# Two attention blocks and a feed-forward on one core: x and context in fp16 parts, a gate buffer of its own, feed-forward in two halves

## The chip, the core and the metric

The kernel runs on one core of a Trainium2 chip. A core has five engines that run their own instruction streams and meet at semaphores: TensorE (matmuls, PE in the profile, its weight loads PEld), VectorE (DVE), ScalarE (ACT), GpSimd (POOL) and SyncE (SP), which here only issues DMAs. The metric is the device time of one launch in microseconds. It is best read as a median of several runs; the profile is one execution of its own.

## What is computed

64 sequences of 128 tokens (x, 320 channels) with a context of 192 channels. Block L0 is attention with 8 heads to the context, plus a small attention over four tokens, with a residual. Block L1 is a transformer layer: self attention with 20 heads, cross attention to the context, and a gated feed-forward.

```python
def L0(x, enc, Wq, Wk, Wv, Wq_ca, Wk_ca, Wv_ca, Wout, b_out):
    keys, ca = enc[:, :-4], enc[:, -4:]
    hs = mha(x @ Wq, keys @ Wk, keys @ Wv)                 # 8 heads
    ca_q1 = einsum('btc,th->bch', ca, Wq_ca)[:, indices]
    ca_hs1 = mha(ca_q1, x, x)
    ca_hs2 = mha(ca_hs1 @ Wq, ca @ Wk_ca, ca @ Wv_ca)
    return (hs + ca_hs2) @ Wout + b_out + x
def L1(x, context):
    h = ln1(x); x = attn(h @ q1, h @ k1, h @ v1) @ o1 + b1 + x     # 20 heads
    h = ln2(x); x = attn(h @ q2, context @ k2, context @ v2) @ o2 + b2 + x
    a, g = split(ln3(x) @ ff_w1 + ff_b1)
    return a * gelu(g) @ ff_w2 + ff_b2 + x
```

## The kernel before

Two sequences (256 columns) make a step; there are 32 steps and a loop of 33 passes (Fori in each engine's block: L475 for SyncE, L587 GpSimd, L805 ScalarE, L1278 VectorE, L1709 TensorE). The passes are a pipeline: pass i does L0 of step i, and the L1 layer of the step before it, and within that feed-forward lags by another part. A tail after the loop does the last feed-forward.

The work is cut into **jobs**, named in the table BODY (L109). A job fills one of six PSUM banks (j_bank, handed round in the table's order), then ScalarE, VectorE or both read it (A, V, AV), and the bank is free for the job six places on. The same order is written out by hand in each engine's loop. Names: Q0T, K0T and V0 project x and context for L0 (three chunks of output channels, or one job per sequence for V), K1T, Q1T, V1 and Q2T, K2T, V2 for L1; Sn are the scores of unit n (four heads), of which VectorE takes maxima; mxg turns the maxima of group g; Tn are the transposed scores less the maxima, of which ScalarE takes two exponentials: P in fp32 (L741) and PT's high part in fp16 (L742). GpSimd forms PT's low part P - PT (low_probabilities, L514), and TensorE's attend n (L1549) multiplies both with V in two other banks. There are 28 units a pass: 0 to 3 the token attention (CA), 4 to 13 self, 14 to 23 cross, 24 to 27 the first attention. P has two slots, PT three (P_SLOTS, PT_SLOTS). outT/outM turn and project an attention's result, followed by residual, statistics, the deviation on GpSimd and norm; XT turns a normed row. fft (t 0 to 9) are the feed-forward's first products, of which ScalarE takes Gelu into gate (L715) and VectorE multiplies into F; y0 and y1 the second product, in parts (ff_part, L1612). G, mT, mB, vca, s4, p4T, hs, caT belong to the token attention and to the scale factors, which are powers of two found afresh in each pass from the largest elements of x and context.

**Precision.** A product in fp16 parts splits both factors into a high and a low part and takes the products high-high, high-low and low-high. With 320 rows of contraction these are eight matmuls (PASSES, L36: the last 64 rows and their low part share one block). Only products of normed rows and weights do so; x and context enter Q0T, K0T, V0, K2T, V2 as fp32: chunk (L1460, through transposed, L1429) takes three fp32 matmuls for x and two for context, values (L1471) two per job. In the trace each fp32 matmul is two instructions.

**Operands on SyncE's queue.** Queries and keys go through DRAM: put writes the two parts of a chunk to a scratch, stack (L373) loads them back with three DMAs, one copy per part pair. SyncE issues in the order of one_pass (L430), and a wait there holds up all that follows. stack_self feeds units 4 to 13, stack_cross_keys and stack_cross_queries units 14 to 23, stack_first_* units 24 to 27. load_next (L423) loads the next step's inputs; cT2 keeps the context for K2T and V2.

**The gate** lies in slot 0 of P (L285). So Gelu 0 waits for the last low part of self attention (L715 and on), and the exponential of unit 14 waits for ff9.

The head (L1143 to L1276 on VectorE) loads and splits the weights, finds their scale, and makes the token attention's products M4.

## Time and profile before

| | us |
|---|---|
| median of 3 runs | 3948.45 |
| lowest, highest | 3946.22, 3966.26 |
| the profiled execution | 3965.49 |
| span of its trace | 3963.6 |
| its mean granted clock | 0.966 |

How to read it: busy time is the union of an engine's instructions. Matmuls are pipelined, so the distance from one start to the next is a matmul's price, and its own length (some 0.2 us for a single one) is not. A granted clock of 1.00 is 2.4 GHz for TensorE and 0.50 is 1.2 GHz. An arrow names what ended an engine's idle time before an instruction.

### The profile page before, as it was taken

The numbers are of one execution on the slowest core, as the hardware profiler recorded it, in microseconds if no ns is written. First come the engines' busy times: TensorE is split into PE (matmuls) and PEld (weight loads), VectorE is DVE, ScalarE is ACT, GpSimd is POOL, SyncE is SP. The second block draws the span as 40 slices with busy tenths as digits, with TensorE's granted clock in tenths as the row PEclk, the third lists the DMA queues.
The fourth block names the chain that finished last, engine by engine and source line by source line (L and its number), as shares of the span: only waits on it lengthen the run. The fifth ranks groups of instructions, "written<-read, shape, count | busy, mean of one in ns | idle before, by whom it ended". The sixth has DMA issues, their size and how long they took to land.

```text
span 3963.6 us, 112057 instructions
## 1 busy us (share of the span) xinstructions
PE 3580.9 (90%) x38314; PEld 2867.6 (72%) x38314; DVE 2308.9 (58%) x5535; ACT 2268.7 (57%) x4084; POOL 1966.4 (50%) x2229
## 2 busy tenths in 40 slices
PE   6499999999999999999999999999999999999999
PEld 5377777777777777777777777777777777777777
DVE  6466556556555655655556556555655656556555
ACT  2356655665556556556655665566566556655664
POOL 0345444554555445555554554545445555554553
PEclk9799999999999999999999999999999999999999
DMA  4332333222233332232333322233332232333321
GB/s 138 63 61 53 58 61 66 59 46 60 59 55 61 67 61 49 53 65 51 63 63 66 59 46 60 56 58 61 67 64 47 53 64 53 63 63 66 59 46 42
DMA packets 417600, 238.71 MB, mean 60 GB/s; under 512 B 44315, under 2 KB 416715, under 8 KB 416843
## 3 DMA queue, kind: packets, MB, share of 16 engines
q1 hardware_dynamic: 405317, 229.62, 29.6%
q8 instruction: 366, 6.00, 0.7%
q10 hardware_dynamic: 11910, 3.04, 0.3%
q14 instruction: 7, 0.06, 0.0%
HBM read 153.50 MB, written 79.06 MB: 59 GB/s over the span
## 4 chain that ended last, share of the span: by engine, by line
PE 36%; issue 30%; POOL 17%; DVE 5%; SPq 4%; DMA 3%; ACT 3%; POOLq 1%; ACTq 0%; DVEq 0%
PE bank L1412 35%; POOL PT L519 10%; DMA xin<-in_x 3%; DVE mx L1025 2%; ACT PT L742 2%; POOL cQ L526 2%; POOL XA L496 1%; POOL cK L526 1%; SPq L365 1%; POOL rstd L566 1%; SPq L363 1%; POOL XB L496 1%; PE bank L1446 1%; PE bank L1531 1%; SPq L361 1%
## 5 line engine op out<-in xcount | busy, mean ns | idle before, releaser
L519 POOL TENSOR_TENSOR PT<-P,PT 128x512 f16<-128x512 f32 (+1 forms) x924 | 1068.8, 1157 | 642.1 <-ACT PT L742 640.8
L1412 PE MATMUL bank<-hT,w_ff_w 128*128 128x256 f16 x5440 | 651.6, 277 | 1.7 <-DVE hT L1054 1.7
L1025 DVE TENSOR_REDUCE mx<-bank 128x4 f32<-128x512 f32 (+1 forms) x924 | 579.6, 680 | 104.4 <-PE bank L1412 96.5
L1412 PEld LDWEIGHTS bank<-hT,w_ff_w 128*128 128x128 f16 x5440 | 532.5, 100 | 73.2 <-issue 6.5
L1412 PE MATMUL bank<-mxs,pick 84*128 84x128 f16 (+1 forms) x3696 | 513.4, 220 | 0.0
L1412 PE MATMUL bank<-w_ff,F 128*128 128x320 f32 x1360 | 411.5, 442 | 1.3 <-DVE F L1104 1.3
L1412 PEld LDWEIGHTS bank<-mxs,pick 84*128 84x128 f16 (+1 forms) x3696 | 375.1, 103 | 16.8 <-issue 8.2
L1412 PEld LDWEIGHTS bank<-V,PT 128*128 128x128 f16 (+1 forms) x9504 | 314.5, 96 | 84.0 <-POOL PT L519 37.9
L723 ACT ACTIVATE P<-bank,ff_b,scale 128x256 f32<-128x256 f32 x340 | 187.8, 562 | 324.9 <-PE bank L1412 285.4
L1412 PE MATMUL bank<-Qs,Ks 96*128 96x128 f16 x2640 | 361.7, 220 | 0.1
L1412 PE MATMUL bank<-V,PT 128*128 128x17 f16 (+1 forms) x9504 | 343.7, 172 | 17.1 <-POOL PT L519 14.3
L1104 DVE SCALAR_TENSOR_TENSOR F<-bank,ff_b,P 128x256 f32<-128x256 f32 x340 | 163.3, 483 | 266.5 <-ACT P L723 262.7
L741 ACT ACTIVATE P<-bank,log_p,held 128x512 f32<-128x512 f32 x330 | 256.2, 776 | 80.7 <-PE bank L1412 42.8
L1412 PEld LDWEIGHTS bank<-w_ff,F 128*128 128x128 f32 x1360 | 242.4, 190 | 78.0 <-DVE F L1104 1.5
L565 POOL TENSOR_TENSOR rstd<-mv,eps 128x1 f32<-128x1 f32 x198 | 41.4, 209 | 502.8 <-DVE mv L1092 502.8
L741 ACT ACTIVATE P<-bank,log_p,exp_self 128x512 f32<-128x512 f32 x330 | 255.6, 775 | 45.0 <-PE bank L1412 42.8
L1412 PEld LDWEIGHTS bank<-Qs,Ks 96*128 96x128 f16 x2640 | 253.2, 98 | 20.9 <-issue 6.0
L1071 DVE RECIPROCAL rden<-bank 128x20 f32<-128x20 f32 (+1 forms) x264 | 63.2, 239 | 345.0 <-PE bank L1412 345.0
L526 POOL TENSOR_TENSOR cQ<-whole,cQ 128x256 f16<-128x256 f32 (+1 forms) x198 | 131.9, 667 | 257.8 <-DVE whole L929 254.2
L741 ACT ACTIVATE P<-bank,log_p,factor 124x512 f32<-124x512 f32 (+1 forms) x264 | 204.9, 776 | 93.4 <-PE bank L1412 87.7
L742 ACT ACTIVATE PT<-bank,log_p,held 128x512 f16<-128x512 f32 x330 | 254.6, 772 | 0.0
L742 ACT ACTIVATE PT<-bank,log_p,exp_self 128x512 f16<-128x512 f32 x330 | 254.4, 771 | 0.0
(274 smaller groups left out, 7295.4 us busy)
## 6 DMA issues: line engine op xcount, KB each, us to landing
Ks<-scratch_k SPq DMA_DIRECT2D x198, 160.0 KB, 4.5
...
cT<-in_cT SPq DMA_DIRECT2D x136, 96.0 KB, 2.0
...
```

The source lines that it names most:

```text
L361: sp.dma_start(cT2[0:r, k, :], d["cT"][before, k * r:(k + 1) * r, :]).then_inc(step_loaded, 16)
L496: nc.gpsimd.tensor_tensor(dst[:, b, :], src[:, b, :], bias[:, j, :], ALU.add).then_inc(ready, 1)
L519: nc.gpsimd.tensor_tensor(PT[0:keys, n % PT_SLOTS, 1, :], P[0:keys, n % P_SLOTS, :], PT[0:keys, n % PT_SLOTS, 0, :], ALU.subtract).then_in ...
L526: nc.gpsimd.tensor_tensor(dst[0:r, 1, k, :], whole[0:r, m % 3, :], dst[0:r, 0, k, :], ALU.subtract)\
L565: link(i, nc.gpsimd.tensor_tensor(rstd[:, j, b:b + 1], mv[:, j, b, 1:2], eps[:, :], ALU.add))
L723: nc.scalar.activation(gate[:, t % 2, :], bank[:, 0:GS], ACT.Gelu, scale=scale[:, 1:2], bias=ff_b[:, FFT + t:FFT + t + 1]).then_inc(a_done, 1)
L741: nc.scalar.activation(P[0:keys, n % P_SLOTS, :], bank[0:keys, :], ACT.Exp, bias=log_p[0:keys, :], scale=by)
L742: nc.scalar.activation(PT[0:keys, n % PT_SLOTS, 0, :], bank[0:keys, :], ACT.Exp, bias=log_p[0:keys, :], scale=by).then_inc(a_done, 1)
L1025: nc.vector.tensor_reduce(mx[:, g % 2, 4 * u:4 * u + 4], bank[:, :].rearrange("p (h s) -> p h s", h=4)[:, :, 0:keys], axis=AX.X, op=ALU.ma ...
L1071: link(i, nc.vector.reciprocal(rden[:, g % 4, 0:heads].unsqueeze(2), o[:, :, e:e + 1]))
L1104: nc.vector.scalar_tensor_tensor(out=F[:, t, :], in0=bank[:, GS:2 * GS], scalar=ff_b[:, t:t + 1], in1=gate[:, t % 2, :], op0=ALU.add, op1= ...
L1412: return nc.tensor.matmul(o, lhsT, rhs, start=start, stop=stop)
```

## The change

It does five things.

- Wq, Wk, Wv, k2 and v2 are loaded and split like the other weights (MATS16). In each pass ScalarE scales x and context by a power of two and takes their high parts (split_x, split_context), GpSimd the low ones (low_x, low_context). Q0T takes eight fp16 matmuls a chunk (PASSES_X), K0T, K2T, V0 and V2 five (PASSES_C). The 64 odd rows stand twice, in two halves of a block. cT2 goes; K2T and V2 read the same c16 as K0T and V0.
- The factors of these jobs' results no longer change from pass to pass: fixed takes the place of factor and next_factor in them.
- gate gets its own buffer, and the two waits between Gelu and the exponentials go.
- Feed-forward: ff0 to ff4 stand between mx0 and K0T1, near the start of the pass, ff5 to ff9 where ff0 to ff9 were.
- Another order of jobs, of TensorE's attends, of GpSimd's additions and of SyncE's queue. load_next stands behind stack_self, extremes_x, extremes_context, mT, mB and next_factors earlier, stack_cross_keys behind stack_cross_queries.

In the head the maxima of the weights are taken in one reduction each instead of two, M4_all shares its memory with raw ff_w1 and is cleared after it, and five weights more are split.

The diff's core (the orders of the other engines follow BODY):

```diff
+MATSX, MATSK = ("Wq",), ("Wk", "Wv", "k2", "v2")
+MATS16 = MATSN + MATSX + MATSK
+BLOCKS = {n: 2 if n in MATSK else 3 for n in MATS16}
+NORM_OF = {"q1": 0, "k1": 0, "v1": 0, "q2": 1, "ff_w1": 2, "Wout": 3, "o1_w": 3, "o2_w": 3,
+           "Wq": 3, "Wk": 3, "Wv": 3, "k2": 3, "v2": 3}
 
 PASSES = ((0, 0, 0), (0, 1, 0), (3, 0, 0), (1, 0, 1), (1, 1, 1), (4, 0, 1), (2, 0, 2), (2, 1, 2))
+
+
+PASSES_C = ((1, 0, 0), (3, 0, 0), (1, 1, 0), (2, 0, 1), (2, 1, 1))
+
+PASSES_X = ((1, 0, 0), (1, 1, 0), (4, 0, 0), (2, 0, 1), (2, 1, 1), (5, 0, 1), (3, 0, 2), (3, 1, 2))
+ROWS_X, AT_X = (64, 128, 128), (128, 0, 192)
...
 BODY = jobs_of("""
-    Q0T0 XT0_0 Q0T1 XT0_1 Q0T2 K1T0 K1T1 K1T2 Q1T0 Q1T1 Q1T2 S0 S1 V0_0 V1_0 mx0 S2 S3 T0 K0T0 T1
-    V1_1 mx1 K0T1 T2 S4 S5 S6 S7 S8 T3 vca mx2 S9 S10 T4 S11 S12 T5 S13 caT0 T6 mx3 T7 T8 caT1 K0T2
-    T9 T10 T11 T12 T13 V0_1 outT1_0 ff0 ff1 outM1_0 outT1_1 ff2 ff3 outM1_1 XT1_0 ff4 s4 XT1_1 ff5
-    Q2T0 Q2T1 Q2T2 ff6 ff7 mT ff8 mB ff9 S14 S15 S16 S17 y1 S18 S19 mx4 S20 S21 S22 T14 S23 K2T0 T15
-    mx5 S24 T16 S25 T17 T18 T19 T20 S26 T21 mx6 T22 outT2_0 S27 y0 T23 p4T T24 mx7 T25 outM2_0 K2T1
-    T26 hs0 T27 outT2_1 V2_0 outT0_0 hs1 K2T2 outM2_1 outT0_1 XT2_0 V2_1 outM0_0 outM0_1 XT2_1 G
+    Q0T0 XT0_0 XT0_1 Q0T1 Q0T2 S0 K1T0 K1T1 K1T2 Q1T0 Q1T1 Q1T2 S1 vca S2 K0T0 S3 mx0 ff0 ff1 T0
+    V1_0 T1 ff2 mx1 ff3 ff4 K0T1 T2 S4 T3 S5 S6 S7 S8 V0_0 mx2 S9 S10 T4 T5 S11 S12 S13 T6 caT0 T7
+    mx3 caT1 T8 V1_1 T9 T10 T11 K0T2 T12 T13 mT outT1_0 V0_1 mB ff5 outM1_0 outT1_1 ff6 outM1_1
+    XT1_0 ff7 K2T0 XT1_1 s4 Q2T0 Q2T1 Q2T2 ff8 ff9 K2T1 K2T2 y1 S14 S15 S16 S17 S18 S19 mx4 S20 S21
+    S22 T14 T15 S23 T16 S24 mx5 T17 S25 T18 T19 T20 T21 S26 T22 S27 p4T T23 mx6 y0 outT2_0 mx7 T24
+    T25 outM2_0 outT2_1 T26 T27 hs0 outM2_1 outT0_0 hs1 V2_0 XT2_0 outT0_1 outM0_0 outM0_1 XT2_1 G
+    V2_1
...
-        gate = P[:, 0, :].rearrange("p (t n) -> p t n", t=2)
+        gate = sb("gate", [128, 2, GS])
...
             def load_next(i):
-                sp.wait_ge(v_done, v_job(i, LOOP_JOBS, "V0_1"))
+                sp.wait_ge(v_done, v_job(i, LOOP_JOBS, "vca"))
+                sp.wait_ge(c16_ready, i + 1)
                 sp.wait_ge(xa_ready, i * G + G)
                 sp.wait_ge(ca_ready, i + 1)
                 sp.wait_ge(vx_ready, i * G + G)
-                load_step(i + 1, i)
+                load_step(i + 1)
 
             def one_pass(i, stores):
-                load_products(i)
                 put_low(i, "Q0T", 0, cQ, CH0, s_q0, AT0, q0_put)
                 put_low(i, "Q0T", 1, cQ, CH0, s_q0, AT0, q0_put)
                 put_low(i, "Q0T", 2, cQ, CH0, s_q0, AT0, q0_put)
                 put_split(i, "K1T", 0, cK, s_k1, self_put)
                 put_split(i, "K1T", 1, cK, s_k1, self_put)
+                load_products(i)
                 put_split(i, "K1T", 2, cK, s_k1, self_put)
                 put_split(i, "Q1T", 0, cQ, s_q1, self_put)
                 put_split(i, "Q1T", 1, cQ, s_q1, self_put)
                 put_split(i, "Q1T", 2, cQ, s_q1, self_put)
                 stack_self(i)
+                load_next(i)
                 put_low(i, "K0T", 0, cK, CH0, s_k0, AT0, k0_put, self_stacked)
-                stack_cross_keys(i)
                 put_low(i, "K0T", 1, cK, CH0, s_k0, AT0, k0_put)
+                stack_first_queries(i)
                 put_low(i, "K0T", 2, cK, CH0, s_k0, AT0, k0_put)
-                load_next(i)
-                stack_first_queries(i)
                 stack_first_keys(i)
                 put_split(i, "Q2T", 0, cQ, s_q2, q2_put, first_stacked)
                 put_split(i, "Q2T", 1, cQ, s_q2, q2_put)
                 put_split(i, "Q2T", 2, cQ, s_q2, q2_put)
                 stack_cross_queries(i)
+                stack_cross_keys(i)
                 put_low(i, "K2T", 0, cK, CH1, s_k2, AT1, k2_put, cross_stacked)
                 put_low(i, "K2T", 1, cK, CH1, s_k2, AT1, k2_put)
                 put_out(i, 0, stores)
+                put_low(i, "K2T", 2, cK, CH1, s_k2, AT1, k2_put)
                 put_out(i, 1, stores)
-                put_low(i, "K2T", 2, cK, CH1, s_k2, AT1, k2_put)
...
+            def low_x(i):
+
+
+                pool.wait_ge(x_high, i + 2)
+                nc.gpsimd.tensor_tensor(x16[:, 3:6, :], xT[:, :, :], x16[:, 0:3, :], ALU.subtract).then_inc(x16_ready, 1)
+
+            def low_context(i):
+
+                pool.wait_ge(c_high, i + 1)
+                nc.gpsimd.tensor_tensor(c16[:, 2:4, :], cT[:, :, :], c16[:, 0:2, :], ALU.subtract).then_inc(c16_ready, 1)
...
+            def split_x(i):
+
+                act.wait_ge(step_loaded, i * LOADS_STEP + 2 * LOADS_STEP)
+                act.wait_ge(next_ready, i + 2)
+                act.wait_ge(j_full, done(i, LOOP_JOBS.number("Q0T2"), "J"))
+                nc.scalar.activation(xT[:, :, :], xT[:, :, :], ACT.Copy, scale=next_factor[:, SX:SX + 1])\
+                    .then_inc(x_scaled, 1)
+                act.wait_ge(x_scaled, i + 2)
+                nc.scalar.activation(x16[:, 0, :], xT[:, 0, :], ACT.Copy, scale=lower[:, :])
+                nc.scalar.activation(x16[:, 1:3, :], xT[:, 1:3, :], ACT.Copy).then_inc(x_high, 1)
+
+            def split_context(i):
+
+                act.wait_ge(step_loaded, i * LOADS_STEP + LOADS_STEP)
+                act.wait_ge(factor_ready, i + 1)
+                act.wait_ge(j_full, done(i - 1, max(LOOP_JOBS.number("K2T2"), LOOP_JOBS.number("V2_1")), "J"))
+                nc.scalar.activation(cT[:, :, :], cT[:, :, :], ACT.Copy, scale=factor[:, SC:SC + 1])\
+                    .then_inc(c_scaled, 1)
+                act.wait_ge(c_scaled, i + 1)
+                nc.scalar.activation(c16[:, 0, :], cT[:, 0, :], ACT.Copy, scale=lower[:, :])
+                nc.scalar.activation(c16[:, 1, :], cT[:, 1, :], ACT.Copy).then_inc(c_high, 1)
...
-                elif t == 0:
-                    act.wait_ge(low_p, units_done(min(i, STEPS) if isinstance(i, int) else i, LAST_UNIT[SELF, 1]))
+                else:
+                    act.wait_ge(v_done, v_job(i - 1, LOOP_JOBS, f"ff{FFT + t - 2}"))
...
-                if n == LAST_UNIT[SELF, 1] + 1:
-                    act.wait_ge(v_done, v_job(i, LOOP_JOBS, f"ff{FFT - 1}"))
...
-            def transposed(bank, wn, rows_k, src, at, r):
-
-                for k, rk in enumerate(rows_k):
-                    last = mm(bank[0:r, 0:GS], w[wn][0:rk, k, at:at + r], src[0:rk, k, :], k == 0,
-                              k == len(rows_k) - 1)
-                return last
-
-            def transposed16(o, wn, src, at, r):
-
-                for x, (blk, part, rows) in enumerate(PASSES):
-                    last = mm(o, w16[wn][:, part, rows, at:at + r], src[:, blk, :], x == 0, x == len(PASSES) - 1)
+            def transposed16(o, wn, src, at, r, passes=PASSES):
+
+                for x, (blk, part, rows) in enumerate(passes):
...
-            def chunk(i, name, c, wn, rows_k, src, at, rows):
-                if name == "K2T":
-                    pe.wait_ge(step_loaded, i * LOADS_STEP + 2 * LOADS_STEP)
+            def chunk(i, name, c, wn, src, passes, at, rows):
+                if c == 0:
+                    pe.wait_ge(x16_ready if src is x16 else c16_ready, i + 1)
                 bank = j_next(i, LOOP_JOBS, f"{name}{c}")
-                transposed(bank, wn, rows_k, src, at[c], rows[c]).then_inc(j_full, 1)
+                transposed16(bank[0:rows[c], 0:GS], wn, src, at[c], rows[c], passes).then_inc(j_full, 1)
...
-            def values(i, name, b, wn, src):
+            def values(i, name, b, wn):
+                if b == 0:
+                    pe.wait_ge(c16_ready, i + 1)
                 bank = j_next(i, LOOP_JOBS, f"{name}_{b}")
-                for k, rk in enumerate(CHC):
-                    last = mm(bank[:, 0:H], src[0:rk, k, b * S:(b + 1) * S], w[wn][0:rk, k, :], k == 0, k == 1)
+                for x, (blk, part, rows) in enumerate(PASSES_C):
+                    last = mm(bank[:, 0:H], c16[:, blk, b * S:(b + 1) * S], w16[wn][:, part, rows, :],
+                              x == 0, x == len(PASSES_C) - 1)
...
-                chunk(i, "Q0T", 0, "Wq", CH0, xT, AT0, CH0)
+                chunk(i, "Q0T", 0, "Wq", x16, PASSES_X, AT0, CH0)
                 turn_norm(i, 0, 0)
-                chunk(i, "Q0T", 1, "Wq", CH0, xT, AT0, CH0)
                 turn_norm(i, 0, 1)
-                chunk(i, "Q0T", 2, "Wq", CH0, xT, AT0, CH0)
+                chunk(i, "Q0T", 1, "Wq", x16, PASSES_X, AT0, CH0)
+                chunk(i, "Q0T", 2, "Wq", x16, PASSES_X, AT0, CH0)
+                scores(i, 0)
                 chunk16(i, "K1T", 0, "k1")
                 chunk16(i, "K1T", 1, "k1")
                 chunk16(i, "K1T", 2, "k1")
                 chunk16(i, "Q1T", 0, "q1")
                 chunk16(i, "Q1T", 1, "q1")
                 chunk16(i, "Q1T", 2, "q1")
-                scores(i, 0)
                 scores(i, 1)
-                values(i, "V0", 0, "Wv", cT)
+                token_values(i)
+                scores(i, 2)
+                chunk(i, "K0T", 0, "Wk", c16, PASSES_C, AT0, CH0)
+                scores(i, 3)
+                turn_maxima(i, 0)
+                ff(i, L, 0)
+                ff(i, L, 1)
+                exponents(i, 0)
                 values1(i, 0)
-                turn_maxima(i, 0)
-                scores(i, 2)
-                scores(i, 3)
-                exponents(i, 0)
-                chunk(i, "K0T", 0, "Wk", CHC, cT, AT0, CH0)
                 exponents(i, 1)
-                attend(i, 0)
-                attend(i, 1)
-                values1(i, 1)
+                ff(i, L, 2)
                 turn_maxima(i, 1)
-                chunk(i, "K0T", 1, "Wk", CHC, cT, AT0, CH0)
+                ff(i, L, 3)
+                ff(i, L, 4)
```

## Rows read from the trace of the kernel before

**Rows 1.** The page, busy time of each engine, share of the span, instructions.
```profile
PE 3580.9 (90%) x38314; PEld 2867.6 (72%) x38314; DVE 2308.9 (58%) x5535; ACT 2268.7 (57%) x4084; POOL 1966.4 (50%) x2229
```
**Rows 2.** Windows E, A, B, C, D: length, PE, PEld, DVE, ACT, POOL, clock, DMA.
```profile
1405.10:1423.66 18.56, 16.77 (x102) 11.22 (x101) 14.29 (x40) 6.70 (x17) 6.06 (x10) 0.91 0.11 32
1423.66:1429.35 5.69, 5.69 (x49) 4.55 (x49) 2.84 (x6) 3.17 (x6) 3.09 (x5) 1.00 0.30 84
1429.35:1465.26 35.91, 30.80 (x423) 24.72 (x422) 18.36 (x40) 24.91 (x42) 19.46 (x19) 0.95 0.46 63
1465.26:1493.16 27.90, 26.78 (x207) 21.96 (x205) 14.62 (x39) 11.64 (x24) 5.67 (x11) 0.94 0.48 109
1493.16:1522.10 28.94, 27.88 (x374) 22.98 (x372) 17.25 (x39) 21.53 (x37) 24.93 (x25) 1.00 0.05 14
```
**Rows 3.** Waits of TensorE, all passes: us in total, times, longest.
```profile
PE bank L1412 <- POOL PT L519: 105.1, 99, 1.6
...
PE bank L1446 <- DVE OB L1098: 28.7, 32, 2.1
```
**Rows 4.** Timeline of TensorE around A: start, us, engine, instruction, count.
```profile
1419.12 2.75 PE L1412 MATMUL bank<-xT,w_Wq 120*120 120x256 f32 x6
1421.68 0.52 PE L1446 MATMUL bank<-ident,OA 128*128 128x128 f32 x3
...
1423.66 2.91 PE L1412 MATMUL bank<-hTn,w_k 128*128 128x256 f16 x24 [0.16 <-DVE hTn L1054]
1426.50 2.91 PE L1412 MATMUL bank<-hTn,w_q 128*128 128x256 f16 x24
...
1429.81 1.29 PE L1412 MATMUL bank<-w_Wv,cT 96*128 96x320 f32 x4
1430.94 1.25 PE L1412 MATMUL bank<-w_v,hTn 128*128 128x320 f16 x8
1432.03 0.27 PE L1531 MATMUL bank<-ident,mx 128*8 128x128 f32 x1
```
**Rows 5.** Windows: the granted clock (before the last two numbers) during Q0T1.
```profile
1419.10:1421.70 2.60, 2.60 (x9) 1.86 (x8) 1.19 (x3) 0.67 (x2) 0.53 (x1) 0.50 0.19 47
```
**Rows 6.** Timeline of ScalarE at the change from Exp to Gelu.
```profile
1463.87 0.50 ACT L699 ACTIVATE hTn<-bank 128x384 f16<-128x384 f32 x1
1464.38 1.28 ACT L723 ACT_TABLE_LOAD   x1
1465.68 1.02 ACT L723 ACTIVATE P<-bank,ff_b,scale 128x256 f32<-128x256 f32 x2
```
**Rows 7.** Timeline of ScalarE, one exponential of 512 elements.
```profile
1453.45 0.76 ACT L741 ACTIVATE P<-bank,log_p,exp_self 128x512 f32<-128x512 f32 x1
```
**Rows 8.** The page, costliest groups: busy, mean ns | idle before, releaser.
```profile
L519 POOL TENSOR_TENSOR PT<-P,PT 128x512 f16<-128x512 f32 (+1 forms) x924 | 1068.8, 1157 | 642.1 <-ACT PT L742 640.8
```
**Rows 9.** Timeline of TensorE in C.
```profile
1466.68 3.66 PE L1412 MATMUL bank<-hT,w_ff_w 128*128 128x256 f16 x32
1470.17 1.25 PE L1412 MATMUL bank<-w_o_w,hTn 128*128 128x320 f16 x8
...
1482.51 3.67 PE L1412 MATMUL bank<-hT,w_ff_w 128*128 128x256 f16 x32
...
1493.16 0.56 PE L1412 MATMUL bank<-Ks,Qs 96*128 96x128 f16 x7
```
**Rows 10.** Timeline of SyncE's queue: issues, start and us of issuing.
```profile
1433.54 1.33 SPq L375 DMA_DIRECT2D Ks<-scratch_k  x3
...
1443.84 0.32 SPq L371 DMA_DIRECT2D scratch_k<-cK  x1
...
1486.78 1.33 SPq L375 DMA_DIRECT2D Qs<-scratch_q  x3
```
**Rows 11.** Timeline of VectorE in the head.
```profile
6.77 5.18 DVE L1170 MEMSET M_all<- 120x6144 f32 x1 [1.22 <-issue]
...
29.63 8.14 DVE L1177 TENSOR_REDUCE amax<-raw_ff_w 128x3 f32<-128x7680 f32 x1
```

More of the change, by code:

```diff
@@ L193, in build @@
         w = {}
-        for n in MATS0:
-            w[n] = sb("w_" + n, [128, 3, H])
         for n in MATSC:
@@ L339, in build @@
         loads = []
-        for n in MATS0 + MATSC:
-            rows = CH0 if n in MATS0 else CHC
-            for k, r in enumerate(rows):
-                loads.append((w[n][0:r, k, :], d[n][sum(rows[:k]):sum(rows[:k]) + r, :]))
+        for n in MATSC:
+            for k, r in enumerate(CHC):
+                loads.append((w[n][0:r, k, :], d[n][k * r:(k + 1) * r, :]))
         for k, r in enumerate(CH0):
@@ L583, in _ @@
             token_queries(-1)
+            low_x(-1)
             assert links[0] == POOL_HEAD_LINKS
@@ L783, in _ @@
             act.wait_ge(scale_ready, 1)
-            for n in MATSN:
-                for k in range(3):
+            for n in MATS16:
+                for k in range(BLOCKS[n]):
                     nc.scalar.activation(w16[n][:, 0, k, :], raw[n][:, k, :], ACT.Copy,
@@ L800, in _ @@
             next_factors(-1, HEAD_JOBS)
+            split_x(-1)
             turn_factors(-1, PER["V"] - 1)
@@ L1354, in _ @@
                 maxima(i, 17)
-                result(i, L, 1)
                 maxima(i, 18)
@@ L1362, in _ @@
                 maxima(i, 23)
-                low_chunk(i, "K2T", 0, cK, CH1[0], FK2)
+                softmax4(i)
+                maxima(i, 24)
                 low_maxima(i, 5)
-                maxima(i, 24)
                 maxima(i, 25)
```

400 lines of the change are left out of this document (206 added, 194 removed).

## The prediction, made before the changed kernel ran

> **What bounds the kernel now.** I read the page first. TensorE is busy 90% of the span, half as much again as any other engine [rows 1], and its weight loads lie under its matmuls. The profiled execution took 3965.5 us (span 3963.6), the median of the three shown is 3948.45: the profiled one is 0.4% above it. I work out a difference and take it from the median.
>
> Next the windows view. One of the 33 passes of the loop is cut at five points of TensorE's own order, which the change keeps: E, from the last exponential of one pass (T27) to K1T0 of the next; A, the six K1T and Q1T products; B, to attend 13; C, to S14; D, to T27. The reader is to see the sum of 117.0 us, and in every row TensorE's busy time against the stretch's length [rows 2]. The waits view of TensorE names who ends its idle time: GpSimd's low parts PT (105 us in 99 waits, in stretch B), and in C the norm in OB before XT1 (28.7 us in 32 waits, 0.9 a pass) [rows 3]. Two things a busy share hides are in the timeline. A is solid TensorE work, 24 fp16 products of 256 columns in 2.84 us, 118 ns each [rows 4]. And after the wait at the end of E the granted clock is half: six fp32 instructions of Q0T1 took 2.56 us in a stretch whose clock is 0.50 [rows 4, 5]; at full clock they are 1.28, so such an episode costs about 1.3 us. B and C have clocks of 0.95 and 0.94 and each hold one as well [rows 2].
>
> So A and C are TensorE-bound, B is a relay between ScalarE, GpSimd and TensorE, E is a VectorE chain (14.3 us of VectorE in 18.6), and D is TensorE with ScalarE close behind [rows 2].
>
> **fp32 products become fp16 ones.** Each fp32 matmul is two instructions in the trace. A V0 job, four instructions of 320 columns, took 1.13 us; eight fp16 ones of 320 columns took 1.09, 136 ns each [rows 4]. Five fp16 products make a new V0 or V2 job: 0.68. Four such jobs a pass: saves 4 x 0.45 = 1.8 us. A Q0T job is six instructions of 256 columns, 1.28 us; eight fp16 products at 118 ns are 0.94: 3 x 0.34 = 1.0. A K0T or K2T job is four of those six, 0.85; five fp16 ones are 0.59: 6 x 0.26 = 1.6. Together 4.4 us a pass less on TensorE, 145 us in 33 passes, if TensorE were the bound in every stretch.
>
> **What the splitting adds.** On ScalarE split_x is one activation of 768 elements and one each of 256 and 512, split_context one of 512 and two of 256. The nearest rows are 0.76 us for 512 elements and 1.02 for two of 256 [rows 6, 7], so about 1.0 for 768: 2.3 + 1.8 = 4.1 us a pass. GpSimd gets low_context (512 elements, 1.16 us by its row of that size [rows 8]) and low_x (768, at most 1.74 in proportion): 2.9 us. split_context sits behind Q0T2 and ahead of K1T0 on ScalarE. In A ScalarE works 3.2 of 5.7 us [rows 2], so it catches up within A. What queues behind it are K1T's high parts, and VectorE's and GpSimd's halves of K1T, then the puts on the SyncE queue; their slack is the same 2.5 us. I take 0, between 0 and +1.8. low_x lies between the low parts of units 23 and 24 in D, where GpSimd is busy 24.9 of 28.9 us; x_values and token_queries (part of that) go to C, so I take +0.5, between 0 and 1.7.
>
> **Feed-forward in two halves.** ff0 to ff4 move from behind attend 9 to the start of B. That needs the gate's own buffer, since it used the P that the exponentials write. Gelu and Exp then alternate: Gelu, Exp, Gelu, Exp in B, Gelu at the start of C, Exp at its end. Before there are two table loads a pass, now six: the load took 1.28 us, began 0.02 us after the activation ahead of it, and Gelu ran 0.02 us after it [rows 6]. Four more are 5.1 us of ScalarE a pass. The Trainium skill, page "ScalarE: Activation LUTs", section "What ACT_TABLE_LOAD costs", adds a drain of about 1.38 us to every switch, and its section "Rules for kernel authors" says to finish one set's functions before switching, which speaks against this change. This trace agrees with the 1283 ns and shows no such drain.
>
> **Stretch by stretch.**
> B (35.9 us). TensorE: 30.8 busy, of which two ff jobs are there already; four more at 1.75 (32 products in 3.49 us [rows 9]) are +7.0; fp16 saves 3 x 0.26 + 2 x 0.45 = 1.7; the half-clock episode, with 1.3, should go, since the waits for PT between units 0 and 3 are now covered by ff. That is 34.8. ScalarE: 24.9 + four loads 5.1 + five Gelus at 0.51 [rows 6] = 32.5. Neither can be full: behind Q1T2's high part ScalarE has nothing until K0T0 (S1, vca, S2 first, about 1.5 us), it waits about 1 us at mx2, and behind its last exponential come 1.16 us of GpSimd and the attend. 32.5 + 4.0 = 36.5: +0.6. So the seven added microseconds of TensorE fit into idle time, and nearly all of the idle time is used up. S4 waits for the stacked queries, whose puts are unmoved; TensorE gets to S4 14.4 us after A, as they land (1443.8 against 1429.4 [rows 2, 10]): 0.
>
> C (27.9 us). It ends when the cross operands are stacked, so I count in two parts. To the end of Q2T2: 1482.5 - 1465.3 = 17.2 us now [rows 2, 9]. Two ff jobs go (3.5), K2T0 comes (0.6), the wait before XT1 (0.9 us [rows 3]; on VectorE the norm stands behind extremes_x, that behind xin's landing) goes because load_next and extremes_x come earlier, but its filler shrinks as well; I take 17.2 - 3.5 + 0.6 - 1.7 = 12.6 with half of the clock episode. From there to S14: the queries are issued 4.27 us after Q2T2 (1486.78 [rows 9, 10]). Before, only they were loaded, three DMAs, and S14 began at 1493.16 without a wait. Now stack_cross_keys stands behind stack_cross_queries on the SyncE queue, so six loads have to land: the self stack, the same six, took 1433.54 to 1443.84, 10.3 us [rows 10]. S14 can start 14.6 us after Q2T2. TensorE's work in between is ff8, ff9, K2T1, K2T2 and all of y1: two ff jobs 3.5, the chunks 1.2, y1's twenty fp32 instructions at 0.28 [rows 4] 5.6, together 10.3. A wait of 4.3 us, for which nothing is queued that could fill it. C = 12.6 + 14.5 = 27.1: -0.8. Without that wait it would be 22.9.
>
> D (28.9 us). TensorE busy 27.9; y1's last eight instructions (2.2) and K2T0, K2T1 (1.7) are gone: 24.0. The start is emptier: S14 to S19 are 1.3 us of TensorE but need six maxima before T14, 2.1 us more of idle. Low_x +0.5. ScalarE has 21.5 less two copies, and cannot start its exponentials before T14 either, so both engines end together near 26.0. The idle 4.3 + 2 us drops the clock as at the end of E: +1.3. 27.3: -1.6.
>
> E (18.6 us). VectorE: 14.3, less K2T2's half 0.5, plus 2.5 of hand-overs (first bank, deviation on GpSimd, XT0_1's turn and high part) = 16.3. XT0_1 now stands ahead of Q0T1, so Q0T1 and Q0T2 cover its split. -2.2.
>
> A: 0. **Sum** +0.6 - 0.8 - 1.6 - 2.2 = -4.0 us a pass, x 33 = -132. The head: one maximum instead of two on ff_w1 saves 8 us (L1177 [rows 11]), 3.4 of it left after five extremes; M4_all's clearing (5.2 [rows 11]) moves from cover onto the path; low_x and split_x stand ahead of the first Q0T0. +2, once. 3948.45 - 130 = 3818 us. TensorE's saved 4.4 us a pass is thus not what the time gets: it is paid out in B and D and given back at S14.
>
> **Rivals.** (1) The wait for the cross operands is short. If six loads land in about six microseconds, S14 has no wait and no clock drop: -4.0 - 4.3 - 1.3 = -9.6, about 3633 us. For it: the queue has fewer loads beside it now, the step's inputs having gone in B. Against it: the self stack had no other loads beside it either.
> (2) Slower: ScalarE's added work in B lies on top of the relay. B's idle time on ScalarE, 11 us, is the relay's own latency (exponential, GpSimd 1.16, attend, next exponential), and P and PT have two and three slots. If none of it can be filled, B is 35.9 + 5.1 + 2.5 = 43.5, +7.6 rather than +0.6: -4.6 + 7.6 = +3.0 a pass, 4049 us. It decides from B = 40.5 on. Against it: the longest idle pieces lie at waits for a bank that TensorE fills late, and there ff now stands.
> (3) A switch costs more than its row. If each drains ScalarE for another 1.28, B gets +5.1 and the pass +1.1: 3986 us. The page named above gives this result by its 2.66 us a switch (estimate from it: +5.5 in B, 3999 us). Against it: 0.02 us on either side of the load [rows 6].
> (4) The splitting gives nothing measurable: gains of D and E go into the same waits for maxima; -1 to +0.5 us a pass, about 3945.
>
> **How the numbers follow.** Chances: forecast (3740 to 3890) 0.50; rival 1 (below 3740) 0.22; between forecast and no change (3890 to 3928) 0.10; rival 4 (3929 to 3968) 0.05; rival 2 0.09; rival 3 0.04. About 0.5% is what a measurement of this kernel can tell from no change. Faster 0.82, same 0.05, slower 0.13. The range, 3650 to 3930, holds the forecast, most of rival 1 and the small gains. It leaves out the slower cases and a pass more than 9 us shorter.
>
> **What would show it.** Windows cut at the same five points: B 36 to 37 us with four table loads in it; C near 27, with a TensorE wait of about 4.3 us at S14 that a DMA into Ks ends; D near 27 with a clock below 1.00 at its start; E near 16. Waits for PT and for hT fall. Products of 256 columns at 118 ns, a V0 job at 0.68 us. Wrong if B is above 40, if S14 does not wait, or if ScalarE idles beside its table loads.

## The result, and the profile after

The changed kernel is slower: median 4082.66 us of 4 runs (4075.25 to 4095.34) against 3948.91 us (3946.22 to 3966.26) beside it, ratio 1.033 with a 95% interval of 1.029 to 1.037. The forecast was 3818 us, faster by 130, with a range of 3650 to 3930. Of all executions below a single one, of e_both_again, was far slower than the others of its kernel (9125.78 us), and its median leaves it out. The profiled execution took 4095.34 us, its span is 4093.5 us, and its mean granted clock is 0.927 where the kernel before had 0.966.

The page after, busy time of each engine, as [rows 1] before:

```profile
PE 3550.5 (87%) x38842; PEld 2916.0 (71%) x38842; DVE 2307.9 (56%) x5551; ACT 2532.6 (62%) x4428; POOL 2059.1 (50%) x2296
```

TensorE is idle for more of the time, and ScalarE has gained some 260 us of work. Neither says where the time went. For that every pass was cut at the five points of the prediction. Below is one pass after (the windows view, columns as in [rows 2]: length, then busy time and count of PE, PEld, DVE, ACT, POOL, the granted clock, DMA share, GB/s); the five lines are A, B, C, D, E.

```profile
759.50:765.20 5.70, 5.70 (x49) 4.56 (x50) 3.75 (x8) 3.96 (x8) 3.63 (x5) 1.00 0.32 85
765.20:805.80 40.60, 36.60 (x489) 31.29 (x489) 21.68 (x48) 32.25 (x51) 19.22 (x19) 0.92 0.51 95
805.80:833.70 27.90, 22.44 (x168) 17.29 (x164) 12.44 (x35) 12.22 (x26) 14.94 (x19) 1.00 0.43 52
833.70:862.70 29.00, 27.72 (x361) 23.93 (x361) 16.70 (x39) 20.97 (x34) 17.30 (x16) 0.82 0.08 24
862.70:877.70 15.00, 12.51 (x104) 8.99 (x104) 12.64 (x37) 5.98 (x16) 6.88 (x11) 1.00 0.04 10
```

D has a clock of 0.82 where [rows 2] has 1.00. Over all passes the windows view gives one line from the first K1T0 to the one 32 passes later, first of the kernel before, then after:

```profile
158.70:3822.80 3664.10, 3375.09 (x36672) 2696.50 (x36672) 2148.91 (x5184) 2166.72 (x3905) 1900.01 (x2150) 0.97 0.30 58
```

```profile
168.60:3948.90 3780.30, 3344.60 (x37187) 2742.38 (x37184) 2153.31 (x5184) 2416.11 (x4226) 1983.18 (x2208) 0.93 0.32 56
```

That is 114.5 us a pass before and 118.1 after, and a loop that begins 9.9 us later. The mean lengths of the stretches, cut in the same way in 31 passes of each trace:

| us a pass | A | B | C | D | E | pass |
|---|---|---|---|---|---|---|
| the pass that the prediction took | 5.7 | 35.9 | 27.9 | 28.9 | 18.6 | 117.0 |
| before, mean | 5.7 | 36.1 | 26.7 | 29.0 | 17.0 | 114.5 |
| forecast | 5.7 | 36.5 | 27.1 | 27.3 | 16.3 | 113.0 |
| after, mean | 5.7 | 39.5 | 28.0 | 30.0 | 15.0 | 118.1 |

The waits view of TensorE after (engine, line waited at, who released it, then us in total, times, longest), to be held against [rows 3]:

```profile
PE bank L1467 <- DMA Ks<-scratch_k: 165.2, 33, 5.7
PE bank L1467 <- DVE whole L1100: 50.0, 33, 3.1
...
PE bank L1467 <- POOL PT L538: 28.1, 61, 0.6
```

The waits for GpSimd's PT are down from 105 us to 28. They were forecast to fall, but part of this fall is TensorE coming late: with the two waits below taken out (e_both) they are 58.5 us in 99 waits. The wait for OB is 10 us instead of 28.7. Two waits are new, each once in every pass. The first is S14's wait for the cross keys, 5.0 us. SyncE's queue shows why (start, length, line, transfer):

```profile
818.59 2.40 SPq L389 DMA_DIRECT2D scratch_q<-cQ  x3
822.46 1.33 SPq L393 DMA_DIRECT2D Qs<-scratch_q  x3
823.91 1.38 SPq L393 DMA_DIRECT2D Ks<-scratch_k  x3
```

The keys have been in memory since the pass before; their stacking is issued at 823.91 only because it stands behind that of the queries. S14 follows at 833.72. The second is K0T2's wait for caT1's bank, 1.5 us a pass. VectorE's timeline (start, length, operation, idle time ahead and what ended it):

```profile
792.15 0.28 DVE L1090 SCALAR_TENSOR_TENSOR mxs<-bank,mxs 20x128 f16<-20x128 f32 x1 [1.46 <-ACT mxs L765]
795.08 0.82 DVE L1007 TENSOR_REDUCE ext_wide<-xin 128x1 f32<-128x640 f32 x1 [2.65 <-DMA xin<-in_x]
795.82 0.41 DVE L1098 COPY whole<-bank 120x256 f32<-120x256 f32 x1
796.15 0.28 DVE L1100 COPY whole<-bank 80x128 f32<-80x128 f32 x1
```

VectorE stands 2.65 us for the landing of the next step's x, which extremes_x wants, with the copy of caT1 queued behind it; TensorE's K0T2 begins at 796.48. Behind it the granted clock is 0.50 (windows view):

```profile
796.40:798.40 2.00, 1.92 (x31) 1.77 (x32) 0.71 (x3) 0.30 (x2) 1.19 (x2) 0.50 0.52 155
798.40:800.40 2.00, 2.00 (x19) 2.00 (x18) 1.40 (x3) 2.00 (x4) 0.63 (x1) 0.50 0.00 0
```

B is 38.2 us in the 13 passes in which its mean clock is 1.00, 40.0 in the 12 with 0.96 and 41.3 in the 7 with 0.92.

### The profile page after: what moved, and what is told of

Same layout as the page of the kernel before. It is cut to its first block, busy times and chain, and to the rows that moved or that the text cites. A ratio compares the mean times of both kernels' runs of the same rounds, so it can differ in the third digit from the quotient of the medians.

```text
span 4093.5 us, 113606 instructions
## 1 busy us (share of the span) xinstructions
PE 3550.5 (87%) x38842; PEld 2916.0 (71%) x38842; DVE 2307.9 (56%) x5551; ACT 2532.6 (62%) x4428; POOL 2059.1 (50%) x2296
## 4 chain that ended last, share of the span: by engine, by line
issue 33%; PE 26%; POOL 23%; DMA 9%; DVE 6%; SPq 2%; ACT 1%; POOLq 1%; DVEq 0%; ACTq 0%
PE bank L1467 23%; POOL PT L538 13%; DMA Ks<-scratch_k 6%; POOL cQ L545 3%; PE bank L1494 2%; POOL cK L545 2%; DMA scratch_q<-cQ 2%; POOL XB L515 2%; SPq L393 1%; DVE mx L1081 1%; POOL c L590 1%; POOL rstd L596 1%; DVE OA L1154 1%; PE bank L1582 1%; POOL XA L515 1%
## 5 line engine op out<-in xcount | busy, mean ns | idle before, releaser
L1467 PE MATMUL bank<-mxs,pick 84*128 84x128 f16 (+1 forms) x3696 | 589.6, 241 | 0.0
L1467 PE MATMUL bank<-Ks,Qs 96*128 96x128 f16 x2640 | 270.8, 265 | 200.5 <-DMA Ks<-scratch_k 165.2
L1467 PE MATMUL bank<-Qs,Ks 96*128 96x128 f16 x2640 | 440.3, 248 | 4.1 <-DVE mxs L1090 3.2
L1467 PEld LDWEIGHTS bank<-mxs,pick 84*128 84x128 f16 (+1 forms) x3696 | 415.8, 115 | 5.3
L1467 PEld LDWEIGHTS bank<-Ks,Qs 96*128 96x128 f16 x2640 | 216.4, 122 | 228.4 <-issue 181.8
L1467 PE MATMUL bank<-V,PT 128*128 128x17 f16 (+1 forms) x9504 | 345.1, 173 | 28.3 <-POOL PT L538 28.1
L1467 PEld LDWEIGHTS bank<-Qs,Ks 96*128 96x128 f16 x2640 | 295.3, 114 | 10.6 <-DVE mxs L1090 7.7
L775 ACT ACTIVATE gate<-bank,ff_b,scale 128x256 f32<-128x256 f32 x340 | 185.8, 561 | 183.6 <-PE bank L1467 95.5
L1160 DVE SCALAR_TENSOR_TENSOR F<-bank,ff_b,gate 128x256 f32<-128x256 f32 x340 | 160.4, 482 | 212.5 <-ACT gate L775 211.3
L765 ACT ACTIVATE mxs<-bank 20x128 f16<-20x128 f32 (+1 forms) x264 | 66.9, 253 | 340.0 <-PE bank L1582 339.5
L982 DVE TENSOR_SCALAR whole<-bank,q_factor,qk_b 128x256 f32<-128x256 f32 (+1 forms) x297 | 160.6, 541 | 147.0 <-ACT cQ L704 111.4
```

Source lines behind the costliest of these rows:

```text
L765: nc.scalar.activation(mxs[0:heads, g % 2, :], bank[0:heads, 0:S], ACT.Copy, scale=2.0 ** -MAX_EXP).then_inc(a_done, 1)
L775: nc.scalar.activation(gate[:, t % 2, :], bank[:, 0:GS], ACT.Gelu, scale=scale[:, 1:2], bias=ff_b[:, FFT + t:FFT + t + 1]).then_inc(a_done, 1)
L982: nc.vector.tensor_scalar(whole[0:r, m % 3, :], bank[0:r, 0:GS], q_factor[0:r, :], qk_b[0:r, c + k:c + k + 1], ALU.mult, ALU.add).then_inc ...
L1160: nc.vector.scalar_tensor_tensor(out=F[:, t, :], in0=bank[:, GS:2 * GS], scalar=ff_b[:, t:t + 1], in1=gate[:, t % 2, :], op0=ALU.add, op1= ...
L1467: return nc.tensor.matmul(o, lhsT, rhs, start=start, stop=stop)
```

## Experiments

The ratios are against the kernel before, run beside them, with 95% intervals. "us a pass" is the difference of medians through 33.

### The two waits, undone one at a time

**e_keys** puts one step of SyncE's queue back towards where it was:

```
                 stack_first_keys(i)
+                stack_cross_keys(i)
                 put_split(i, "Q2T", 0, cQ, s_q2, q2_put, first_stacked)
...
                 stack_cross_queries(i)
-                stack_cross_keys(i)
```

> The changed kernel with one step of SyncE's queue put back: the stacking of the cross keys stands behind that of the first keys, ahead of the puts of Q2T, instead of behind the stacking of the cross queries. Theory Q (the queue): S14's wait of 4.9 us a pass goes, and with it most of the 20 us at the granted clock of 0.50 that follow it; 4 to 8 us a pass, 32 passes, so 3830 to 3955 us. Theory W (the other engines' work sets the pass, and the wait only shows it): the time stays at 4060 to 4090 us and TensorE waits elsewhere in D. If only the wait goes and the clock stays at 0.50 behind S14, about 3930 to 3990.

Measured: 3897.49 us (3881.61 to 3921.93), ratio 0.987 (0.982 to 0.992), which is 185 us less than the changed kernel, 5.6 a pass. C fell from 28.0 to 23.1 us and D from 30.0 to 28.7. The stacking is now issued in B's last microseconds, long before it is needed. Theory Q holds. Most of the gain is the wait itself, 4.9 us. D gives 1.2, less than "most of the 20 us at half clock" would have been worth: its clock is still 0.88 in 21 of 32 passes, and TensorE now stands about 2 us ahead of mx4, where it stood 1 us.

**e_ext** moves one instruction of VectorE:

```
-                extremes_x(i + 1)
                 copy_hT(i, "caT1", 1, CH0)
                 low_part(i, "V1", 1, V1, HEADS1, D1, V1_FACTOR)
                 normalise(i, 2)
+                extremes_x(i + 1)
                 extremes_context(i + 1)
```

> The changed kernel with one instruction of VectorE moved: the largest magnitude of the next x is taken just ahead of that of the next context, behind the copy of caT1, V1_1's low part and normalise 2, instead of ahead of them. Theory V (VectorE stands for the landing of x while caT1's bank is wanted for K0T2): the 3.1 us wait ahead of K0T2 goes and with it the short stretch at half clock; B falls from 39.5 us to about 37, 1.5 to 3 us a pass, so 3985 to 4035 us. Theory A (ScalarE's added work in B: splits, Gelu and table loads): B's length is set by ScalarE, TensorE waits for it a little later, and the time stays within 15 us of 4083.

Measured: 4033.76 us (4031.0 to 4037.72), ratio 1.020 (1.0175 to 1.0225): 49 us less than the changed kernel, 1.5 a pass, at the high edge of what was expected. B fell from 39.5 to 37.9, and its clock is 1.00 in 30 of 32 passes, where it was 1.00 in 13. So most of what this wait cost was the half clock behind it: B at a clock of 1.00 was 38.2 us already.

**e_both** has both edits.

> Both edits, e_keys and e_ext, in the changed kernel. If both causes are right and independent, the gains add: 3780 to 3900 us, faster than the kernel before. Theory W or A: within 30 us of the better one of the two alone.

Measured: 3829.83 us (3823.87 to 3835.98), ratio 0.969 (0.966 to 0.972); the same kernel once more, **e_both_again** (below), took 3819.12. Two moved lines turn the change from 3.3% slower to 3.1% faster than the kernel before. Together they give 253 us, 7.7 a pass, where the two alone add up to 7.1. One pass of it, A to E:

```profile
719.00:724.70 5.70, 5.65 (x48) 4.55 (x48) 3.74 (x8) 4.05 (x8) 3.54 (x5) 1.00 0.32 87
724.70:762.40 37.70, 34.25 (x490) 29.39 (x490) 21.89 (x48) 32.19 (x51) 19.31 (x19) 1.00 0.54 97
762.40:785.30 22.90, 22.33 (x167) 17.27 (x163) 11.87 (x34) 12.21 (x26) 12.35 (x16) 1.00 0.42 72
785.30:814.30 29.00, 26.59 (x362) 22.87 (x361) 17.16 (x40) 21.04 (x34) 19.89 (x20) 0.88 0.08 24
814.30:829.30 15.00, 12.52 (x104) 8.99 (x104) 12.64 (x37) 5.98 (x15) 6.88 (x11) 1.00 0.04 10
```

C is 22.9 us with TensorE busy for 22.3 of them: almost nothing is left to wait for.

### The same order in the kernel before

**b_keys** is the kernel before with stack_cross_keys moved behind stack_cross_queries and nothing else.

```
                 put_low(i, "K0T", 0, cK, CH0, s_k0, AT0, k0_put, self_stacked)
-                stack_cross_keys(i)
...
                 stack_cross_queries(i)
+                stack_cross_keys(i)
```

> The kernel before with this one part of the change: the stacking of the cross keys is put behind that of the cross queries. Theory Q: S14 now waits for its keys as in the changed kernel, some 4.4 us a pass later (27.0 us from K0T2's region less the 26.7 of before are not enough: S14 stood 15.5 us behind Q2T2 in the changed kernel, and Q2T2 ends 16.0 us into C here, so C would be 31.5 against 26.7), and the clock falls to 0.50 behind it, 1 to 3 us more: 4.4 to 7.5 us a pass, 4090 to 4190 us. Theory W: 3940 to 3980 us.

Measured: 4160.6 us (4158.1 to 4166.73), ratio 1.053 (1.050 to 1.056), 6.4 us a pass. This one line costs the kernel before more than the whole change did. Its TensorE waits have the same new entry,

```profile
PE bank L1412 <- DMA Ks<-scratch_k: 126.7, 33, 4.2
```

3.8 us a pass, and a pass near its mean shows the rest, C then D:

```profile
2610.50:2640.60 30.10, 25.30 (x207) 21.08 (x206) 14.64 (x39) 11.63 (x24) 9.49 (x16) 0.98 0.62 117
2640.60:2672.20 31.60, 30.53 (x373) 24.80 (x373) 17.32 (x39) 21.59 (x37) 21.14 (x19) 0.91 0.05 14
```

Its means are 30.3 us for C (26.7 before) and 31.2 for D (29.0 before, at a clock of 1.00 in [rows 2]). So 2.2 us of the 6 lie behind the wait, in a stretch whose work hasn't changed.

**b_gate** is the kernel before with the gate's own buffer alone: `gate = sb("gate", [128, 2, GS])`.

> The kernel before with this one part of the change: the gate has a buffer of its own instead of a slot of P. No view of the kernel before shows a wait for that slot, and the order stays. Every theory: within 0.3% of the kernel before, 3940 to 3960 us.

Measured: 3945.15 us (3940.21 to 3952.32), ratio 0.999 (0.998 to 1.001). The buffer costs and gives nothing by itself.

### ScalarE's tables

**e_both_nosw** is e_both with `ACT.Identity if jobs is LOOP_JOBS and t < 5 else ACT.Gelu` for the Gelu.

> The kernel with both edits (cross keys' stacking ahead, extremes_x behind), and in it the Gelu of ff0 to ff4 of each pass is left out: the instruction stays, but with Identity for Gelu, so that ScalarE's tables don't switch between Gelu and Exp in B (4 of the 6 loads of a pass, 5.2 us of ScalarE's time; that part of the result is wrong). Theory T (the loads and what waits behind them are what is left of B, 37.8 us against 36.1 in the kernel before): B falls by 1.5 to 4 us a pass, 3700 to 3780 us. Rival (the loads stand in slack, as forecast): within 0.6 us a pass, 3810 to 3835 us.

Measured: 3809.32 us (3804.97 to 3826.82), ratio 0.966 (0.963 to 0.970), 20.5 us or 0.6 a pass below e_both. B is 37.6 us against 37.8, although ScalarE has 4.9 us less to do in each pass. The gain lies for the most part in D (27.8 against 28.3), where no load was taken away; how often the clock falls there differs between two executions of the same kernel too (below). So B is not set by ScalarE's sum: each load takes the 1.28 us of its row and stands in slack. The time is just below the 3810 to 3835 us that the rival (loads in slack) expected, and far above the 3780 of Theory T. ScalarE's timeline after, where Gelu and Exp alternate:

```profile
776.68 1.28 ACT L775 ACT_TABLE_LOAD   x1
777.98 0.56 ACT L775 ACTIVATE gate<-bank,ff_b,scale 128x256 f32<-128x256 f32 x1
778.44 0.25 ACT L765 ACTIVATE mxs<-bank 8x128 f16<-8x128 f32 x1
778.60 1.06 ACT L775 ACTIVATE gate<-bank,ff_b,scale 128x256 f32<-128x256 f32 x2
779.55 0.47 ACT L713 ACTIVATE cK<-bank,fixed 120x256 f16<-120x256 f32 x1
780.16 1.28 ACT L791 ACT_TABLE_LOAD   x1
```

The load begins 0.14 us after the copy ahead of it has ended, and Gelu follows one 0.02 us behind its end. The drain of about 1.38 us that the Trainium skill ("ScalarE: Activation LUTs", "What ACT_TABLE_LOAD costs") adds to a switch isn't there in these rows either, now with six switches a pass.

### What the clock takes

Behind S14's wait the clock is at its lower level. Windows of 2 us after; the first two are the wait, S14 starts in the third:

```profile
829.70:831.70 2.00, 0.00 (x0) 0.00 (x0) 0.00 (x0) 0.00 (x0) 1.60 (x3) 1.00 1.22 108
831.70:833.70 2.00, 0.00 (x0) 0.00 (x0) 0.00 (x0) 0.00 (x0) 0.00 (x0) 1.00 0.09 8
833.70:835.70 2.00, 1.98 (x20) 1.99 (x21) 1.37 (x3) 0.00 (x0) 0.00 (x0) 0.52 0.46 131
...
837.70:839.70 2.00, 2.00 (x21) 2.00 (x20) 1.79 (x4) 0.27 (x1) 0.00 (x0) 0.50 0.04 8
...
843.70:845.70 2.00, 2.00 (x49) 2.00 (x47) 0.96 (x2) 1.90 (x4) 1.58 (x2) 0.92 0.00 0
845.70:847.70 2.00, 2.00 (x51) 2.00 (x48) 0.68 (x1) 2.00 (x4) 1.49 (x2) 1.00 0.03 8
```

Behind S14 TensorE is busy in all but one of these windows (0.96 of 2.00 us at 835.70, ahead of mx4, not shown), at half speed for about 10 us; in 8 of the 32 passes it is about 20 us, and D is then over 30 us. **e_fill** keeps the wait and takes away the standing still: 40 products ahead of it into S14's bank.

```
                 if (b, u) == (0, 0):
+                    if att == CROSS:
+                        n14 = LOOP_JOBS.number(f"S{n}")
+                        bank_free(i, LOOP_JOBS, n14)
+                        for _ in range(40):
+                            mm(j_bank[n14 % J_BANKS][:, 0:GS], w16["ff_w1"][:, 0, 0, 0:128], hT3[:, 0, :])
```

> The changed kernel as it is, its wait for the cross keys kept, but TensorE is given 40 products of 256 columns (109 ns each, 4.4 us in all) to do ahead of S14 in the 4.9 us that it stood still; they go into S14's bank, which S14 overwrites, so the result is unchanged. Theory C (the 20 us at the granted clock of 0.50 in D come from TensorE's standing still): S14 starts at the same time, but D runs at a clock near that of the kernel with the keys' stacking put forward (0.88 to 0.94 in D) and takes 28.7 us instead of 29.96, some 40 us in all: 4030 to 4055 us. Rival: the clock falls in D for another reason (the short products of S14 to S22, the 1.0 us wait ahead of mx4): 4075 to 4095 us.

Measured: 4058.48 us (4044.72 to 4065.13), ratio 1.027 (1.024 to 1.030), 24 us below the changed kernel, just short of what was expected. D fell from 30.0 to 28.4 us; 20 of 32 passes take less than 28.2 us in D, where in the changed kernel none is below 28.8. C is as long as before (28.1). B rose by 0.45 us, for no cause that the trace shows, so a pass is only 1.0 us shorter in the trace (117.1 us) and 0.7 by the medians. So TensorE's standing still does bring its clock down here, and useless work ahead of the wait was worth more than none.

**e_warm** does the same in e_both: 18 products into mx4's bank, where TensorE stands for 2.3 us behind S19.

```
                 bank = j_next(i, LOOP_JOBS, f"mx{g}")
+                if g == 4:
+                    for _ in range(18):
+                        mm(bank[:, 0:GS], w16["ff_w1"][:, 0, 0, 0:128], hT3[:, 0, :])
```

> The kernel with both edits, and 18 products of 256 columns (109 ns each, 2.0 us) that TensorE does into mx4's bank in the 2.3 us in which it stands ahead of mx4; the turning of the maxima overwrites them, the result is unchanged. In the kernel with both edits the granted clock is 0.50 for 13 us behind that wait in the pass looked at, 0.79 to 0.94 in D from pass to pass. Theory C (TensorE's standing still brings the clock down, and the half clock costs time in D): D's clock is 1.00 and D falls from 28.31 us to 27.0 to 27.7, 0.6 to 1.3 us a pass, 3785 to 3812 us. Rival: the clock follows the short products around the wait or the half clock is hidden by ScalarE's chain in D: 3820 to 3840 us.

**e_head** moves low_x(-1) on GpSimd, ahead of the loop, from behind token_queries(-1) to ahead of x_values(-1).

> The kernel with both edits, and ahead of the loop GpSimd makes x's low part before the values and token queries of the first step instead of behind them; TensorE waited for it once, 7.7 us. Expected: that wait goes, part of it may come back as a wait for the first token queries or G; 2 to 7 us in all, 3822 to 3830 us, too little for the times to show, so it is read in the trace from the start of the first K1T0.

Measured: e_warm 3810.5 us (3805.09 to 3823.39), ratio 0.964 (0.962 to 0.967); e_head 3812.38 (3811.2 to 3813.9), ratio 0.965 (0.963 to 0.968). Both are lower than e_both, e_head by far more than its edit can give, and below the 3822 to 3830 us expected of it. In its trace the wait of 7.7 us is gone, 3.4 us come back as one for the token queries, and the first K1T0 starts 1.8 us earlier. So some 15 of the 17 us were spread. e_warm's time lies in the range of Theory C, but not by its mechanism: the wait ahead of mx4 is filled (D's waits for maxima fell from 2.1 to 0.5 us a pass) and the clock is 1.00 in 26 passes, yet no pass has a D below 27.7 us, as in e_both, where most passes have 0.94. So the short drop of the clock that most passes of e_both have costs nothing in D. And D's mean is 28.2 us against e_both's 28.3, because in 6 of 32 passes the clock falls later than before, 10 us behind S14 (which starts in the first window), though TensorE never stood for long:

```profile
1661.40:1663.40 2.00, 2.00 (x31) 1.92 (x31) 1.84 (x4) 0.00 (x0) 1.87 (x3) 1.00 0.49 139
1663.40:1665.40 2.00, 1.75 (x18) 1.35 (x17) 2.00 (x4) 0.00 (x0) 0.78 (x1) 1.00 0.00 0
1665.40:1667.40 2.00, 2.00 (x36) 1.83 (x34) 1.89 (x5) 0.80 (x2) 0.00 (x0) 1.00 0.00 0
1667.40:1669.40 2.00, 1.47 (x22) 1.12 (x19) 1.93 (x5) 2.00 (x4) 1.01 (x1) 1.00 0.00 0
1669.40:1671.40 2.00, 1.69 (x36) 1.36 (x36) 1.00 (x3) 2.00 (x5) 1.60 (x3) 1.00 0.00 0
1671.40:1673.40 2.00, 1.85 (x20) 1.86 (x21) 0.76 (x2) 2.00 (x4) 1.68 (x2) 0.62 0.00 0
```

To separate the edits from the spread, **e_warm_head** (both small edits on e_both) and **e_both_again** (e_both unchanged) were timed beside each other.

> The kernel with both edits and with both of the last two small ones, the 18 products ahead of mx4 and x's low part ahead of the first step's values. Alone they measured 3810.5 and 3812.4 us, with both edits only the kernel measured 3829.8 us, in another call. If those 17 to 19 us belong to the two edits and add: 3790 to 3800 us. If they are the spread of the clock in D from one execution to the next (the traces show 27.7 us in most passes of all three, and one fall of the clock or another in 5 to 9 passes): 3805 to 3815 us, the same as the kernel with both edits beside it.

> The kernel with both edits once more, on the chip and in the rounds of the one before, to compare the two. If the 3829.8 us hold: 3825 to 3835 us. If the difference from 3811 was spread: 3805 to 3822 us.

Measured: e_warm_head 3806.5 us (3804.2 to 3821.54), ratio 0.964 (0.962 to 0.967); e_both_again 3819.12 us (3808.34 to 3829.15), ratio 0.967 (0.964 to 0.969). Both are what was expected if the difference was spread. The intervals overlap: 13 us between them is a hint and no more. In their traces 2 passes of 32 have a half clock of note in D (over 28.2 us) against 6. The best version is thus one of the e_both family, 3.1 to 3.6% faster than the kernel before.

### A repair that failed

**e_y1**, on e_both, puts y1's last four products back between S17 and S18, to give TensorE work in that 2.3 us wait.

```
                 scores(i, 17)
+                ff_part(i, 1, 6, 10)
                 scores(i, 18)
```

(with y1 behind S17 in the list of jobs, its drain behind maxima 17, and K2T2 ahead of y1's first part.)

> The kernel with both edits, and the last four products of y1 (6 to 9) put back between S17 and S18, as in the kernel before, with K2T2 ahead of y1's first part for the sake of the banks. In the kernel with both edits TensorE stands for 2.3 us ahead of mx4 (VectorE's maxima of S14 to S18 take longer than TensorE's units), and the clock in D is 0.79 to 0.94. Theory M: the wait becomes work (four products, 2.1 us), and the clock in D rises to 0.94 or more: 2 to 3.5 us a pass, 3720 to 3770 us. Rival: D is set by the exponentials and their maxima on VectorE, the two us come back as waits for T14's bank or its maxima: 3815 to 3835 us.

Measured: 3863.89 us (3861.01 to 3865.61), ratio 0.978 (0.976 to 0.981), 34 us slower than e_both; both expectations were wrong. TensorE's timeline there:

```profile
1449.77 3.50 PE L1467 MATMUL bank<-w_ff,F 128*128 128x320 f32 x12 [0.44 <-DVE cK L988]
1454.83 1.06 PE L1467 MATMUL bank<-Ks,Qs 96*128 96x128 f16 x16 [1.56 <-DMA Qs<-scratch_q]
```

C is 23.1 us as before. From Q2T2's end to the landing of the queries' stack it takes 10.6 us whatever TensorE does meanwhile, so the 2.1 us of work taken out of C left a wait for Qs, and of the work put into D 1.2 us show in its length (28.3 to 29.5). The four products stood in the right place: ahead of S14, covering the relay of the queries.

## Why the prediction was wrong, point by point

The sum was -4.0 us a pass, the traces show +3.65. The miss is 265 us: the difference of 7.65 us, times 33, makes 252 of them, the head 8, and the rest is rounding and the spread between executions. No single step failed. The largest are a base read from one pass, VectorE's wait for the next x in B that was put at nothing, and D's work and clock, sized too small.

**The base: 2.5 us.** The stretches were read from one pass of 117.0 us [rows 2]. The mean is 114.5: E is 17.0, not 18.6, and C 26.7, not 27.9. That pass held half-clock episodes in C and E that most don't: C's clock is below 0.95 in 12 of 32 passes, E's in 6. The gains forecast for C and E, 0.8 and 2.2, were in part the difference between this pass and a usual one. One division would have shown it, 3664.1 us between two K1T0 by 32. A third of the miss is this step.

**B: 3.0 us (39.5 against 36.5).** The forecast took ScalarE's 32.5 us plus 4.0. ScalarE is busy 32.3 us, as forecast, but it isn't what sets B: e_both_nosw took 4.9 us off it and B moved by 0.2. Half of the 3.0 is extremes_x, which the prediction named twice, as an early step that helps C, and never put in VectorE's queue in B: it waits for a transfer there, and caT1's bank waits for it. e_ext priced it at 1.5 us a pass. Most of that is the clock: "the half-clock episode, with 1.3, should go" was wrong, it is there in 19 of 32 passes and in 2 of e_ext. The other 1.3 to 1.5 us remain in e_both (B 37.8), where TensorE waits 3.5 us a pass in B, 1.8 of them for PT and 0.6 for the stacked queries; none of these waits was tested by itself, so this part stays open. Rival 2 gave the nearest time, 4049 us, by ScalarE's loads and Gelus on top of the relay; that it is near is luck, since B stays below its 40.5 and it is wrong as a cause. The absorption it doubted happened for the most part: TensorE's own work in B, counted with each instruction at the interval it has in undisturbed places, rose from 26.7 to 32.1 us, and in e_both B grew by 1.7.

**C: 0.9 us (28.0 against 27.1).** To Q2T2's end 12.5 us, forecast 12.6. From there to S14 15.5 us, forecast 14.5: the wait for the cross keys is 5.0 us where 4.3 was written. The mechanism, its place and the transfer that ends it were right. The prediction priced it at 4.3 us and 1.3 for the clock, 5.6 a pass; taking it out gave 5.6 (e_keys). This cost stood in the sum at about its right size; the gains set against it did not.

**D: 2.7 us (30.0 against 27.3).** The prediction's own terms, 24.0 us of work, 2.1 of idling and 0.5 for low_x, add up to 26.6, and it went on with 26.0. Most passes of e_both take 27.7 us in D, with TensorE busy for 25.3 and waiting about 2.1 for maxima. The idling was thus right and the work 1.3 us too small, most of it outM2_1 (eight products of 320 columns, 1.1 us): it stood in E before and stands in D now, and the prediction counted its move in neither. The clock was put at 1.3, and is 30.0 - 27.7 = 2.3. The prediction took it from the episode in E [rows 4, 5], which lasts about 3 us (a clock of 0.91 in 18.56 us [rows 2]); behind S14 it lasts 10 or 20.

**E: -1.3 us (15.0 against 16.3).** Better than forecast; outM2_1's move to D, 1.1 us of TensorE's work, is probably most of it and then no gain of the pass (not tested). With XT0_1 ahead of Q0T1 the wait for its result, 1.6 us a pass before, is gone, and no pass after has a half clock in E.

**The head: +10 us, forecast +2.** TensorE waits once for x's low part, 7.7 us, and once for the scaled x, 6.7. "low_x and split_x stand ahead of the first Q0T0" was written and given no number. Its waits for the bias (ff_b) and for the maxima's row are 6.3 and 3.3 us longer too, and the waits for the other maxima 10.7 us shorter.

**What held.** fp16 saves TensorE 4.5 us a pass (its own work, counted as above, fell from 96.6 to 92.1), forecast 4.4. The splits took 2.0 and 1.6 us on ScalarE, 1.64 and 1.15 on GpSimd (forecast 2.3, 1.8, 1.74, 1.16). Four more table loads at 1.28 us, with no drain: rival 3 is false. Rival 1, a short wait at S14, is false as to the queue as written; with the keys' stacking moved (e_both) it is the state reached, and it is 3829.8 us, not 3633, since the other terms above don't go away. The gate's buffer costs nothing (b_gate). Net of the two waits the change is worth 119 us, 3.6 us a pass, against 4.5 saved on TensorE. No run has the fp16 parts or the split feed-forward alone, so how these 3.6 us divide between them and the new order isn't shown.
